# Products with B of a selective scan, moved from VectorE to TensorE for all of the first scan and a quarter of the later ones

## The reference

```
proj = x @ in_proj; hidden, gate = split(proj)          # 512 channels each
u = silu(conv4(hidden)); dt, B, C = split(u @ x_proj)   # B, C: 16 states per token
B, C, dt = rms(B), rms(C), rms(dt); dt = softplus(dt @ dt_proj + b)
s[t] = exp(dt[t] * A) * s[t-1] + (dt[t] * u[t]) * B[t]  # 512 channels x 16 states
y[t] = sum over states of s[t] * C[t]; y = (y + u*D) * silu(gate); out = y @ out_proj
```

## Time and profile before

| | |
|---|---|
| three runs | 2929.85, 2920.2, 2906.3 us; median 2920.2 |
| the profiled execution | 2907.69 us, its span 2905.9 us |
| mean granted TensorE clock | 0.867 |
| PE, DVE, ACT, POOL busy | 2377.7, 2143.5, 1367.2, 659.6 us |
| period of a middle turn | about 293 us |

### The profile page before, as it was taken

One profiled execution on the slowest core, in us unless ns is written; L12 is line 12 of the kernel. 1 busy time (PEld: TensorE's weight loads), 2 busy tenths in 40 slices (PEclk: granted clock), 3 DMA queues, 4 the chain that ended last, 5 costly groups with the idle time before them and its releaser, 6 DMA issues.

```text
span 2905.9 us, 36704 instructions
## 1 busy us (share of the span) xinstructions
PE 2377.7 (82%) x12295; PEld 1450.7 (50%) x12295; DVE 2143.5 (74%) x3034; ACT 1367.2 (47%) x2186; POOL 659.6 (23%) x611
## 2 busy tenths in 40 slices
PE   4457798988888888988898889788879787887991
PEld 2345345544554455545544554445445543556880
DVE  4998975798589857995889598958795751246666
ACT  4437254725572556354735474547443416153440
POOL 2202000411050115011420132203310313035661
PEclk7568698969996999699968997999789888998995
DMA  3322230213221322132213221321132164374757
GB/s 121 118 84 81 81 106 24 74 63 113 68 83 56 121 71 71 53 122 84 71 63 112 84 64 55 124 87 46 63 105 95 44 152 147 98 236 145 223 176 305
DMA packets 140614, 297.05 MB, mean 102 GB/s; under 512 B 14464, under 2 KB 83600, under 8 KB 140176
## 3 DMA queue, kind: packets, MB, share of 16 engines
q1 hardware_dynamic: 126608, 256.15, 27.1%
q0 software_dynamic: 13824, 38.55, 3.6%
HBM read 225.11 MB, written 69.54 MB: 101 GB/s over the span
## 4 chain that ended last, share of the span: by engine, by line
PE 48%; DVE 23%; ACT 12%; issue 9%; POOL 4%; DMA 3%; SPq 0%; DVEq 0%; POOLq 0%; ACTq 0%
PE bank L2164 10%; DVE scan L1597 7%; PE bank L2372 5%; PE bank L2177 4%; PE bank L2311 4%; PE bank L2327 3%; DVE scan L1606 3%; PE bank L2291 3%; PE bank L2660 3%; DVE rest L1753 2%; ACT rest L1354 2%; PE bank L2398 2%; PE bank L2681 2%; PE bank L2151 2%; ACT scan L1310 2%
## 5 line engine op out<-in xcount | busy, mean ns | idle before, releaser
L1597 DVE TENSOR_TENSOR_SCAN scan<-scan 128x1024 f32<-128x1024 f32 x256 | 593.6, 2319 | 48.9 <-ACT scan L1310 45.5
L1310 ACT ACTIVATE scan<-scan 128x511 f32<-128x511 f32 x512 | 338.9, 715 | 424.7 <-DVE scan L1597 416.3
L2291 PE MATMUL bank<-ident,scan 128*128 128x128 f32 x2048 | 323.9, 314 | 147.4 <-DVE scan L1606 137.9
L2291 PEld LDWEIGHTS bank<-ident,scan 128*128 128x128 f32 x2048 | 276.6, 163 | 216.5 <-DVE scan L1606 127.1
L1621 DVE TENSOR_TENSOR scan<-scan 128x1024 f32<-128x1024 f32 x256 | 313.8, 1226 | 14.0 <-DMA scan<-bc_dram 5.9
L1606 DVE TENSOR_TENSOR scan<-scan 128x1024 f32<-128x1024 f32 x256 | 318.4, 1244 | 1.7 <-DVE rest L1788 1.3
L991 POOL DMA_INDIRECT rows_dram<-stage,slot_at x128 | 186.1, 1454 | 562.1 <-DVE chosen L1700 390.2
L2372 PE MATMUL bank<-rest 32*128 32x384 f32 (+3 forms) x1024 | 271.1, 641 | 30.0 <-DVE rest L1753 29.1
L969 POOL TENSOR_SCALAR rs<-mv 128x4 f32<-128x4 f32 x24 | 20.9, 870 | 986.6 <-DVE off L1522 985.9
L1354 ACT ACTIVATE rest<-bank 128x2048 f32<-128x2048 f32 (+3 forms) x128 | 158.1, 1235 | 142.9 <-PE bank L2398 142.7
L1753 DVE TENSOR_REDUCE rest<-bank 128x2 f32<-128x1024 f32 (+3 forms) x176 | 195.1, 1122 | 36.4 <-PE bank L2377 34.4
(11 more groups left out here) (391 smaller groups left out, 4281.8 us busy)
## 6 DMA issues: line engine op xcount, KB each, us to landing
scan<-bc_dram SPq DMA_DIRECT2D x256, 512.0 KB, 3.7
wslot<-wt SPq DMA_DIRECT2D x64, 384.0 KB, 3.2
rows_dram<-scan SPq DMA_DIRECT2D x32, 670.0 KB
scan<-y_dram SPq DMA_DIRECT2D x32, 512.0 KB, 10.0
rest<-rows_dram SPq DMA_DIRECT2D x108, 134.0 KB, 2.5
scan<-rows_dram SPq DMA_DIRECT2D x52, 134.0 KB, 2.8
scan<-wt SPq DMA_DIRECT2D x4, 1536.0 KB, 16.0
wslot<-x SPq DMA_DIRECT2D x8, 512.0 KB, 3.8
```

Of the source, the lines that this page charges most:

```text
L1310: i = a.activation(decay[:, unit % 2, n, 1:], dt[:, c, 1:], ACT.Exp, scale=a_neg[:, c, 2 * pair + n:2 * pair + n + 1])
L1597: d.tensor_tensor_scan(flat, decay[:, unit % 2].rearrange("p n t -> p (n t)"), flat, 0.0, ALU.mult, ALU.add).then_inc(decay_used.sem, 1)
L2291: m = t_.matmul(A.bank(("yT", c))[:, t * P:(t + 1) * P], drive[:, unit % NDRIVE, n, t * P:(t + 1) * P], ident[:, :], is_transpose=True, st ...
```

## The change

`PE_DRIVES = 32, 8`: PE makes the drives of all 32 units of the first scan and of the first 8 units of each later scan, 88 of 256. DVE keeps the others. For a drive on PE:

- `turn_dtu`: PE transposes two tiles of dt*u (8 transposes into two banks) and ACT copies them into SBUF as `dtu_T`; twice in the first scan, once in each later one.
- `diagonals`: for each load and state ACT writes four 128x128 diagonal matrices, the identity scaled by B of 128 tokens (`b_tok`, a new small DVE operation), into the half of the `bc` slot that held B; 16 loads in the first scan, 4 in each later one. The broadcast loads of B for these units are gone.
- `drive_product`: 8 f32 matmuls of 128x128, dtu_T times the diagonals, put the drive into two PSUM banks: banks 2 and 3 or 4 and 5 in turn in the first scan; banks 6 and 7 in a later one, so that each product waits for the scan of the unit before. DVE's scan reads the drive from PSUM and writes to SBUF.

New waits: the rank product of the routing and PV's first step wait for the scan of unit 7 of the next turn, which frees banks 6 and 7; `turn_dtu` waits until the last two gates and the router's product have been taken from these banks; the first load of B for DVE waits for the PE products that used its slot.

```diff
+PE_DRIVES = 32, 8
...
+            def turn_dtu(turn, c):
+
+                act.wait_ge(dtu_turning, dtu_turned_at(turn, c))
+                b = pe_drive_banks(turn, 0)
+                a.activation(dtu_T(turn, c), b[:, (c % 2) * SEQ:(c % 2 + 1) * SEQ], ACT.Copy).then_inc(dtu_turned, 1)
+
+            def diagonals(turn, load, n):
...
+                for t in range(NT):
+                    i = a.activation(diag_of(load)[:, n, t], ident[:, :], ACT.Copy, scale=b_tok[:, turn % 2, t, state:state + 1])
+                i.then_inc(diag_ready, 1)
...
+                    if unit < by_pe(turn):
+                        dve.wait_ge(driven, made(turn, unit + 1))
...
+                if ring is K and by_pe(late + 2):
+                    pe.wait_ge(decay_used.sem, decay_used.at(late + 2, by_pe(late + 2)))
...
+            def turn_dtu(turn, two):
...
+                    else:
+                        handed(G.given_back(turn, ("gate", NCT - 2)), G.given_back(turn, ("gate", NCT - 1)))
+                        if turn >= 2:
+                            handed(K.given_back(turn - 2, ("rt", 0)))
...
+            def drive_product(turn, unit):
...
+                before = unit - (1 if turn else 2)
+                if before >= 0:
+                    pe.wait_ge(decay_used.sem, decay_used.at(turn, before + 1))
+                if unit % 2 == 0:
+                    pe.wait_ge(diag_ready, made(turn, unit) + 2)
+                for n in range(2):
+                    for t in range(NT):
+                        m = t_.matmul(b[:, n * SEQ + t * P:n * SEQ + (t + 1) * P], dtu_T(turn, c)[:, t * P:(t + 1) * P], diag_of(load)[:, n, t], start=True, stop=True)
+                m.then_inc(driven, 1)
...
+                                if turn + 1 < BATCH and by_pe(turn + 1):
+                                    pe.wait_ge(decay_used.sem, decay_used.at(turn + 1, by_pe(turn + 1)))
```

More of the change, by code:

```diff
@@ L209, in unit_of, with by_pe, made, by_dve @@
     return u // 2, u % (2 * NPAIR) // 2, tile
+def by_pe(turn):
+    return PE_DRIVES[1 if turn else 0]
+def made(turn, n, all_of=by_pe):
+    return sum(all_of(t) for t in range(turn)) + n
+def by_dve(turn):
+    return NU - by_pe(turn)
 def weave(columns, order):
@@ L565, in build, with dtu_T, diag_of @@
         gmod = area(16, SEQ)
+        def dtu_T(turn, c):
+            return xnT[:, c] if turn else area(16 + c, SEQ)
+        def diag_of(load):
+            return bc[:, load % 2, 0].rearrange("p n (t q) -> p n t q", t=NT)
         tanhT = area(17, SEQ)
@@ L698, in build @@
         bc_out = Signal(sem("bc_out"), 16)
-        bc_in = [[Signal(sem(f"{n}_in{i}"), 16 * NPAIR) for i in range(2)] for n in "bc"]
+        b_in = [sem(f"b_in{i}") for i in range(2)]
+        c_in = [Signal(sem(f"c_in{i}"), 16 * NPAIR) for i in range(2)]
         decay_ready = Signal(sem("decay_ready"), NU)
         decay_used = Signal(sem("decay_used"), NU)
-        drive_ready = Signal(sem("drive_ready"), NU)
+        drive_ready = sem("drive_ready")
+        driven, diag_ready, dtu_turning, dtu_turned = (sem(n) for n in ("driven", "diag_ready", "dtu_turning", "dtu_turned"))
         unit_done = Signal(sem("unit_done"), NU)
@@ L748, in build, with pe_drive_banks, dtu_turned_at @@
         x3_dram = nc.dram_tensor("x3_dram", [BATCH, SEQ, HID], F32).ap()
+        def pe_drive_banks(turn, unit):
+            first = 6 if turn else 2 + 2 * (unit % 2)
+            return psum[:, first * 512:(first + 2) * 512]
+        def dtu_turned_at(turn, c):
+            return (sum(min(by_pe(t), 2) if t else by_pe(0) // NPAIR // 2 * 2 for t in range(turn)) if turn else 0) + c + 1
         def marked(name, k):
@@ L803, in units_in @@
                     pair, slot = load % NPAIR, load % 2
-                    for g, used in enumerate((drive_ready, unit_done)):
+                    own = load - by_pe(turn) // 2
+                    if own >= 0:
                         yield
-                        if load >= 2 or turn:
-                            sp.wait_ge(used.sem, used.at(turn, 2 * load - 2))
-                        sp.dma_start(bc[:, slot, g], rows[g, 2 * pair:2 * pair + 2, :].partition_broadcast(P)).then_inc(bc_in[g][slot].sem, 16)
+                        if own >= 2 or (turn > 1 and load < 2):
+                            sp.wait_ge(drive_ready, made(turn, 2 * own - 2, by_dve))
+                        elif load < 2:
+                            sp.wait_ge(driven, made(turn, 2 * load - 2))
+                        else:
+                            sp.wait_ge(driven, made(turn, 2 * load - 2))
+                        sp.dma_start(bc[:, slot, 0], rows[0, 2 * pair:2 * pair + 2, :].partition_broadcast(P)).then_inc(b_in[slot], 16)
+                    yield
+                    if load >= 2 or turn:
+                        sp.wait_ge(unit_done.sem, unit_done.at(turn, 2 * load - 2))
+                    sp.dma_start(bc[:, slot, 1], rows[1, 2 * pair:2 * pair + 2, :].partition_broadcast(P)).then_inc(c_in[slot].sem, 16)
             def rest_io(turn):
@@ L1291, in units @@
             def units(turn):
+                if by_pe(turn):
+                    yield
+                    if turn == 0:
+                        act.wait_ge(consts, 1)
+                    for c in range(2):
+                        turn_dtu(turn, c)
+                    for n in range(2):
+                        yield
+                        diagonals(turn, 0, n)
                 for unit in range(NU):
+                    if unit == 14 and unit + 2 < by_pe(turn):
+                        yield
+                        for c in range(2, NCT):
+                            turn_dtu(turn, c)
                     yield
                     decay_unit(turn, unit)
+                    if unit % 2 == 0 and unit + 2 < by_pe(turn):
+                        for n in range(2):
+                            yield
+                            diagonals(turn, unit // 2 + 1, n)
                     if unit in (2 * NPAIR, 2 * NPAIR + 1):
@@ L1554, in front_part @@
                 s = fv.step(d.tensor_tensor(ssm[:, :, 0:DTRANK], ssm[:, :, 0:DTRANK], bc2(a_ss[:, 0:NT], DTRANK), ALU.mult).then_inc(fv.sem, 1))
+                if turn >= 2:
+                    dve.wait_ge(driven, made(turn - 1, 0))
+                marked("b_tok", fv.step(d.tensor_tensor(b_tok[:, turn % 2], ssm[:, :, DTRANK:DTRANK + NSTATE], bc2(a_ss[:, NT:3 * NT:2], NSTATE), ALU.mult).then_inc(fv.sem, 1)))
                 for g in range(2):
@@ L1585, in units @@
                 uv.n = 0
-                drive_unit(turn, 0)
+                if by_pe(turn) == 0:
+                    drive_unit(turn, 0)
                 for unit in range(NU):
@@ L1593, in units @@
                     yield
-                    dve.wait_ge(drive_ready.sem, drive_ready.at(turn, unit + 1))
-                    dve.wait_ge(decay_ready.sem, decay_ready.at(turn, unit + 1))
-                    flat = drive[:, unit % NDRIVE].rearrange("p n t -> p (n t)")
-                    d.tensor_tensor_scan(flat, decay[:, unit % 2].rearrange("p n t -> p (n t)"), flat, 0.0,
-                                         ALU.mult, ALU.add).then_inc(decay_used.sem, 1)
-                    if unit + 1 < NU:
+                    if unit < by_pe(turn):
+                        dve.wait_ge(driven, made(turn, unit + 1))
+                        if unit >= NDRIVE or turn:
+                            dve.wait_ge(unit_summed.sem, unit_summed.at(turn, unit - NDRIVE + 1))
+                    else:
+                        dve.wait_ge(drive_ready, made(turn, unit - by_pe(turn) + 1, by_dve))
+                    dve.wait_ge(decay_ready.sem, decay_ready.at(turn, unit + 1))
+                    if unit < by_pe(turn):
+                        flat = drive[:, unit % NDRIVE].rearrange("p n t -> p (n t)")
+                        d.tensor_tensor_scan(flat, decay[:, unit % 2].rearrange("p n t -> p (n t)"), pe_drive_banks(turn, unit), 0.0,
+                                             ALU.mult, ALU.add).then_inc(decay_used.sem, 1)
+                    else:
+                        flat = drive[:, unit % NDRIVE].rearrange("p n t -> p (n t)")
+                        d.tensor_tensor_scan(flat, decay[:, unit % 2].rearrange("p n t -> p (n t)"), flat, 0.0,
+                                             ALU.mult, ALU.add).then_inc(decay_used.sem, 1)
+                    if by_pe(turn) <= unit + 1 < NU:
                         yield
@@ L1603, in units @@
                     if unit % 2 == 0:
-                        dve.wait_ge(bc_in[1][load % 2].sem, bc_in[1][load % 2].at(turn, 16 * (load // 2 + 1)))
+                        dve.wait_ge(c_in[load % 2].sem, c_in[load % 2].at(turn, 16 * (load // 2 + 1)))
                     dve.wait_ge(decay_used.sem, decay_used.at(turn, unit + 1))
@@ L1614, in drive_unit @@
                 if unit % 2 == 0:
-                    dve.wait_ge(bc_in[0][load % 2].sem, bc_in[0][load % 2].at(turn, 16 * (load // 2 + 1)))
-                if unit % (2 * NPAIR) < 2:
```

(48 more changed lines are left out.)

13 lines of the change are left out of this document (added), and 143 rows, old and new, of the table ORDER.

## The result

The changed kernel took 3041.77 us (median of 4 runs, 3038.25 to 3051.38), the kernel before 2917.81 beside it: a ratio of 1.0432, 95% interval 1.0403 to 1.0461. It is slower by 124 us. The forecast was 2945, its range ended at 3030.

The account below looks back on a forecast made before the run. DVE alone was taken to bound the first scan, other stages to have different limits. First part -36, six later turns +48 and rest 0 +14 gave +26 on 2907.69, 2934; with the median's 12.5 offset, 2945 us, range 2862 to 3030.

Parts of the forecast that it names:

- stage B: Scores and row maxima of a later turn, 57.6 us: more scans and products with C lengthen it, +15.5 us a turn.
- A with E to G: Norm, q, k, v (-4 us); linear attention and next front part (-4 us): a later turn shortens as DVE units leave.
- C: Softmax and values, 60.7 us, full on DVE: holds units 10 to 22 before and after, so 0.
- D: MLP, 56.4 us, PE alone: three units go there under PE's cover, +0.5 us a turn.
- First part: Start through first scan and the stretch after: -35.5 + 7 - 8 = -36 us, bounds -10 to -50.
- The stretch behind it: Between 226 and 283 us, after the first scan: loses six units of scan 1, taken as -8 us, bounds 0 and 19.
- Rest 0: Turn of rest 0: six more scans and products with C, two drives fewer, +18 - 4 = +14 us.
- The clock: PE's granted clock, the least certain term: products are full-height matmuls, so it was let rise; B had 0.64.
- Rival 1: Slower: clock stays low in B, +25 us instead of +15.5, first scan gains 17; total 3030; chance 0.17.
- Rival 2: Faster: DVE sets E to G, -15.5 us a turn instead of -4; total 2865; chance 0.28.
- rival 3: The waits bite: rank product and turnings hold PE's queue 2 us a turn, +14, total 2960; chance 0.10.

Follow-up runs that it names:

- the shifted order: Kernel before, scan steps from the score stage's first unit on four units later in turns 1 to 6: 3011.03 us; with filler among the scores 3066.01 us.

## Why the prediction was wrong

Two terms of the sum for a later turn failed: stage B, where the product was let hide and the wait for it was put at nothing, and A with E to G, where I took 8 us a turn back for DVE work that leaves, and hardly any came.

- **Stage B, +15.5 a turn; +22.0 measured.** The sign, the place and the kind of cost were right (DVE units moved into a full stage), the size was not. In turn 3 DVE's busy time in B went from 53.16 to 69.56 us, +16.4 against the +14.5 that I counted, and its idle time from 4.4 to 9.7, +5.3 against +1.0. Over turns 1 to 6 it is +17.2 and +4.7; B held 4.5 scans before and 10.3 after, not five and ten. Of the idle time 4.00 us is one wait for product 0, which I had as a bound and not in the sum. PE first stood for the diagonals, then made this product in 3.76 us, as the clock was still low:

```profile
1244.03 3.76 PE L2415 MATMUL bank<-scan 128*128 128x128 f32 x16 [1.20 <-ACT scan L1381]
...
1247.83 2.29 DVE L1689 TENSOR_TENSOR_SCAN scan<-scan,bank 128x1024 f32<-128x1024 f32 x1 [4.00 <-PE bank L2415]
```

  Two choices were wrong. As nearest row for the product I took the sum of the earlier trace rows, 1.04 us for 8 of 128x128, but a sum is made of transposes and a drive of f32 matmuls, and these show two instructions each: 2.05 us. The page of before had it: the up projection is 64 products of two f32 matmuls, 128 in all, and its row says x256 (a transpose of the sum, 256 x 8 in all, stands as x2048). I also added PE's work up over the stage, where the single pair of banks puts each product in series with the scans around it. Half the product alone would still not have saved it (1.9 of the 22.0 came back), as DVE's path is as long. The row of the page of before:

```profile
L2164 PE MATMUL bank<-hT,wslot 128*128 128x512 f32 x256 | 119.7, 604 | 0.0
```

- **A and E to G, -8 a turn; -0.2 measured (-1.9 in turns 1 to 5).** I allowed a GpSimd step, a sum and some waits on DVE to come back. The experiment with 17.6 us less DVE work there gave 1.7. The GpSimd step did get shorter, from 2.90 to 1.01 us, but not for the reason that I read out of the earlier trace rows: beside its short step DVE isn't idle but takes a norm's statistics, and so it does beside the step of the changed kernel (the line of before first):

```profile
1441.57 1.40 DVE L1516 BATCH_NORM_STATS2 t_stats<-xb 128x6 f32<-128x256 f32 x4
...
1514.17 1.40 DVE L1598 BATCH_NORM_STATS2 t_stats<-xb 128x6 f32<-128x256 f32 x4
...
1514.74 1.01 POOL L1012 TENSOR_TENSOR rs<-rs,minus_half 128x4 f32<-128x4 f32 x1
```

  So this step came off and little of it shows in the stretch. I take it that the waits and steps that I counted are on a path next to others as long, with PE working 102 us of 119; no run takes these paths apart. The two terms together are +6.5 and +7.8, C adds 2.9 that I had at 0, and D took 0.8 off where I had +0.5: 24.0 a turn instead of 8, of which six turns make 96 us of the error.
- **First part, -36; -18.6 measured.** Where nothing else is on PE the scans came 3.5 us apart, as worked out (3.35 and a short wait), with the high clock; scan 0 was 8.8 us later (7 taken). But the scan's end moved by 13.8 only, where 28.5 was forecast: DVE, which should have been full, was busy 123.98 of 149.0 us, and waited for products in the gaps where PE has other work. Two scans 3.52 us apart, and the waits up to 175 us:

```profile
75.00 2.28 DVE L1689 TENSOR_TENSOR_SCAN scan<-scan,bank 128x1024 f32<-128x1024 f32 x1
...
78.52 2.28 DVE L1689 TENSOR_TENSOR_SCAN scan<-scan,bank 128x1024 f32<-128x1024 f32 x1
...
DVE scan L1689 <- PE bank L2415: 14.4, 4, 4.7
...
DVE scan L1689 <- ACT scan L1392: 2.8, 2, 1.5
```

  The stretch behind it gave 4.8 instead of 8.
- **Rest 0, +14; +18.4 measured**: B +22 where I had +18, E to A -8.7 where I had -4.
- **Turn 7, left out; -12.7 measured.** The prediction never looked at the end of the order.
- **The clock** rose in B as I let it (0.64 to 0.77 in turn 3; in the first scan 0.63 to 0.94). It went with the products and not with the transposes, as in the earlier trace rows: in the same order without later products, where the sums remain, it was 0.56.
- **The rivals.** Rival 1's 3030 lies near the result for a reason that did not happen. Rival 2 is refuted by experiment. Of rival 3 a part came: at the rank product PE waited for the scan in four turns, 5.7 us in all, where rival 3 had 2 us a turn. Diagonals cost 389 ns each instead of 251, and were hidden in B but for the first of a turn:

```profile
PE bank L2313 <- DVE scan L1689: 5.7, 4, 1.7
```

The range failed although B's bound of +20 held the wait for product 0: its upper end was made from a low clock alone, and even there A and E to G give 8 us a turn back and C costs nothing.

## What to carry to other kernels

Before work is moved to another engine, ask where its buffers allow it to run: if that place is a stage where the old engine is full, the move can cost more than the work that it saves. Price a new instruction from a row of the same kind (matmul, not transpose) and, if it has one buffer, add it to the path from consumer to consumer, not to its engine's total. DVE work taken from a stretch that it doesn't set is worth next to nothing: here 1.7 us out of 17.6.

## What the runs showed that I had not expected

A filler that kept the clock at 1.00 through the last turn's scores did not in a middle turn: its clock in B was 0.70 in the shifted order, after waits of 1.1 and 1.7 us. With the filler in the old order the kernel was 0.9% slower, and B 1.9 us longer on average, though PE's clock there was higher.
